# Attention on one core: context, input and weights transposed by the host, all batches written out, and a new spread of the projection steps

## The reference, cut to what matters

```python
# x [16, 256, 128], ctx_768 [16, 1601, 96]; 16 heads of 8
def self_attention(x, qkv_w, out_w, out_b):        # stage 1, keys = the batch's own 256 rows
    ...
    return jnp.einsum('bne,fe->bnf', out, out_w) + out_b
def cross_attention(x, context, ...):              # stages 2 and 5, keys = 1601 rows of the context
    q = x @ Wq.T + bq ; k, v = split(context @ Wkv.T + bkv)
    att = softmax(einsum('blhd,bmhd->blmh', q, k) * scale, axis=2)
    out = einsum('blmh,bmhd->blhd', att, v).reshape(b, l, d)
    return out @ Wo.T + bo
x = layernorm(x + self_attention(x))
x = layernorm(x + cross_attention_0(x, ctx_768))
x = layernorm(x + experts(x))
x = layernorm(x + state_space(x))
x = layernorm(x + cross_attention_1(x, ctx_768))
x = layernorm(x + feed_forward(x))
```

## Time and profile before

| | us |
|---|---|
| median of 3 runs | 4210.55 (4205.43 to 4215.28) |
| the profiled execution | 4211.14 |
| its span | 4209.1 |
| PE busy (matmul) | 3603.7 (86%) |
| DVE busy | 2896.4 (69%) |
| ACT busy | 2384.8 (57%) |
| POOL busy | 1032.1 (25%) |
| mean share of the 16 DMA engines, queue q1 | 19.7% |

### The profile page before, as it was taken

The page is one execution under the profiler, slowest core; times in us unless marked ns, Lnnn a source line. Parts: engine busy times, 40 slices in busy tenths (PEclk is TensorE's granted clock), DMA queues, the critical chain, the costliest instruction groups (busy, mean ns, idle before and its releaser), DMA issues. The chain is left out here.

```text
span 4209.1 us, 109822 instructions
## 1 busy us (share of the span) xinstructions
PE 3603.7 (86%) x39651; PEld 1800.8 (43%) x39651; DVE 2896.4 (69%) x3938; ACT 2384.8 (57%) x4687; POOL 1032.1 (25%) x1818
## 2 busy tenths in 40 slices
PE   4777599999999999997699583999999999999987
PEld 2444244343343434443466482443444334344435
DVE  4555677777777777784544696777777777777753
ACT  2444266666666666675233440666666666666663
POOL 3333232122222321221366102122212212221200
PEclk7889699999999999998799796999999999999998
DMA  2222222222222223221000002222222222222200
GB/s 73 57 54 53 58 56 55 68 60 53 60 51 51 56 53 73 59 50 27 1 0 0 1 0 49 59 51 56 56 69 60 52 60 50 52 55 67 55 21 20
DMA packets 222502, 200.19 MB, mean 48 GB/s; under 512 B 86918, under 2 KB 184444, under 8 KB 221964
## 3 DMA queue, kind: packets, MB, share of 16 engines
q1 hardware_dynamic: 221964, 193.04, 19.7%
HBM read 25.59 MB, written 2.10 MB: 7 GB/s over the span
## 5 line engine op out<-in xcount | busy, mean ns | idle before, releaser
L627 ACT ACTIVATE cross_Pr<-cross_sT 128x512 f32<-128x512 f32 (+1 forms) x3584 | 1833.4, 563 | 886.1 <-PE cross_sT L542 884.5
L691 DVE TENSOR_REDUCE cross_nm<-cross_ring 128x2 f32<-128x802 f32 x2048 | 1974.6, 991 | 492.5 <-PE cross_ring L508 482.7
L542 PE MATMUL cross_sT<-cross_Q,cross_K 64*128 64x256 bf16 x13312 | 1050.8, 274 | 111.3 <-ACT cross_Pr L627 40.7
L561 PE MATMUL cross_oT<-cross_Pr,cross_V 128*9 128x256 f32 x13312 | 1038.7, 383 | 0.6 <-issue 0.6
L542 PEld LDWEIGHTS cross_sT<-cross_Q,cross_K 64*128 64x128 bf16 x13312 | 514.1, 95 | 869.3 <-ACT cross_Pr L627 694.7
L508 PE MATMUL cross_ring<-cross_K,cross_Q 64*128 64x401 bf16 x4096 | 666.4, 338 | 38.3 <-DVE cross_nm L691 17.2
L436 POOL TENSOR_TENSOR cross_mp<-cross_nm,cross_one 128x8 bf16<-128x8 f32 x128 | 26.0, 203 | 1471.0 <-DVE cross_nm L696 1470.8
L561 PEld LDWEIGHTS cross_oT<-cross_Pr,cross_V 128*9 128x9 f32 x13312 | 198.4, 88 | 427.7 <-issue 247.3
L508 PEld LDWEIGHTS cross_ring<-cross_K,cross_Q 64*128 64x128 bf16 x4096 | 200.5, 94 | 170.6 <-DVE cross_nm L691 113.7
L700 DVE TENSOR_REDUCE self_nm<-self_ring 128x4 f32<-128x1024 f32 x128 | 156.7, 1224 | 141.2 <-PE self_ring L515 141.1
L1243 DVE TENSOR_TENSOR moe_rc<-moe_r,moe_bank 128x512 f32<-128x512 f32 x128 | 87.9, 687 | 169.3 <-ACT moe_r L1134 169.3
(11 more groups left out here) (326 smaller groups left out, 3370.8 us busy)
## 6 DMA issues: line engine op xcount, KB each, us to landing
cross_K<-cross_kparts SPq DMA_DIRECT2D x1152, 100.1 KB, 2.3
cross_C<-in_ctx_dram SPq DMA_DIRECT2D x32, 576.0 KB
cross_Q<-cross_qparts SPq DMA_DIRECT2D x288, 64.0 KB, 2.1
self_Q<-self_qparts SPq DMA_DIRECT2D x144, 64.0 KB, 2.1
self_K<-self_kparts SPq DMA_DIRECT2D x144, 64.0 KB, 2.1
cross_xs<-X SPq DMA_DIRECT2D x32, 128.0 KB, 2.1
X<-in_x_dram SPq DMA_DIRECT2D x4, 512.0 KB, 6.1
self_xs<-X SPq DMA_DIRECT2D x16, 128.0 KB, 2.1
```

The lines of the kernel that those rows point to most:

```text
L542: mm = pe.matmul(sT[0:r, cfg.sT_bank(rb, u + j), (c % 2) * S:(c % 2 + 1) * S], K[ROWS * j:ROWS * (j + 1), pair, t, s:s + r], Q[ROWS * j:RO ...
L561: mm = pe.matmul(oT[32 * j:32 * j + VR, 0:S], V[0:r, rb % VB, c, 4 * g + j, :], Pr[0:r, slot, (c % 2) * S:(c % 2 + 1) * S], start=(c == 0) ...
L627: act.activation(Pr[0:r, u % NPR, 0:nc_ * S], sT[0:r, cfg.sT_bank(rb, u), 0:nc_ * S], ACT.Exp).then_inc(exped, 1)
L691: dve.tensor_reduce(nm4[:, g % 2, t, :, pk, blk], R.rearrange("p (j n) -> p j n", j=2)[:, :, 0:cfg.block], AX.X, ALU.max, negate=True).the ...
```

## The change

1. **Layouts.** The host hands in `x_T` [16, 128, 256] and `ctx_T` [16, 97, 1601] (96 rows of the transposed context and a row of ones) and the weights already permuted, with the bias rows of K and V appended. `CT`, the tiles `C`, `cT`, `xs` and the turning of weights are gone. `LOAD_C` is one DMA of 97 x 1601 floats into one of two buffers `in0`, `in1`; each row is 6404 bytes, and on both sides the access pattern is 97 rows by 1601 elements. `LOAD_C` of batch b waits for `V` of batch b-2. `wk` and `wv` of the cross stages arrive as 97 x 128. `XT` is left in the cross stages only, and reads X directly; in self, Q, K and V are computed from `in`.
2. **Output bias.** L584's matmuls are gone. The bias is loaded on all 128 partitions, and GpSimd adds it to X in a step `BIAS` (one tensor_tensor of 128 x 256 per batch); `OUT` waits for it.
3. **Written out.** The hardware loop is gone, and all iterations are written out.
4. **Self.** Q's and K's parts share one tile, and STACK_Q and STACK_K are one set of 9 DMAs of 128 KB. Q and K of a batch move to steps -2s-4 and -2s-3, the STACK to -2s; `A` stays at -s.
5. **Cross schedule.** `A`, `MT` and `ROWS` are one step earlier; K at 9, 11, 13 (was 9, 10, 11), V at 48, 52, 55 (was 28, 31, 34), Q at 4, STACK_K at 27, 30, 44, s+1 (was 26, 30, 44, s+1), `LOAD_C` at 27 as before.

The diff, cut to its core:

```diff
-            self.loop = (1, B - 3, 2)
...
-                out += [(g * u - u - 5 + a * u // 16, ("A", g, a)) for a in range(16)]
-                out += [(g * u - 3, ("MT", g)), (g * u - 2, ("ROWS", g))]
-            out += [(-s + 1 + n, ("CT", n)) for n in range(3)]
-            out += [(-s + 5, ("XT", 0)), (-s + 7, ("Q", 0)), (-s + 7, ("SPLIT_Q",))]
-            out += [(-s + 9 + n, ("K", n)) for n in range(3)]
...
-            out += [(-s + 28 + 3 * n, ("V", n)) for n in range(3)]
-            out += [(-s + 13, ("STACK_Q",))]
-            out += [(-s + at, ("STACK_K", g)) for g, at in enumerate((26, 30, 44, s + 1))]
-            out += [(-2 * s + 27, ("LOAD_X",)), (-2 * s + 27, ("LOAD_C",))]
-            end = 3
+                out += [(g * u - u - 6 + (a * u + 2) // 16, ("A", g, a)) for a in range(16)]
+                out += [(g * u - 4, ("MT", g)), (g * u - 3, ("ROWS", g))]
+            out += [(-s + 1, ("XT", 0)), (-s + 4, ("Q", 0)), (-s + 4, ("SPLIT_Q",)), (-s + 12, ("STACK_Q",))]
+            out += [(-s + at, ("K", n)) for n, at in enumerate((9, 11, 13))]
...
+            out += [(-s + at, ("V", n)) for n, at in enumerate((48, 52, 55))]
+            out += [(-s + at, ("STACK_K", g)) for g, at in enumerate((27, 30, 44, s + 1))]
+            out += [(-2 * s + 27, ("LOAD_C",))]
+            bias, ox, ont, fin, ln = 2, (32, s + 3), s + 5, s + 7, s + 9
...
-            out += [(-2 * s, ("XT", 0)), (-2 * s + 1, ("Q", 0)), (-2 * s + 1, ("SPLIT_Q",)), (-2 * s + 2, ("K", 0)),
-                    (-2 * s + 2, ("SPLIT_K", 0)), (-2 * s + 4, ("V", 0)), (-3 * s + 4, ("LOAD_X",)),
-                    (-2 * s + 3, ("STACK_Q",)), (-2 * s + 3, ("STACK_K", 0))]
-            end = 2
+            out += [(-2 * s - 4, ("Q", 0)), (-2 * s - 4, ("SPLIT_Q",)), (-2 * s - 3, ("K", 0)),
+                    (-2 * s - 3, ("SPLIT_K", 0)), (-2 * s + 2, ("V", 0)), (-3 * s - 3, ("LOAD_X",)),
+                    (-2 * s, ("STACK_K", 0))]
+            bias, ox, ont, fin, ln = 0, (2 * u + 2, 4 * u + 2), s + 4, s + 6, s + 7
...
-        C = sb("C", [P, NCHK, DC], F32) if cfg.cross else None
-        cT = sb("cT", [DC + 1, NK], F32) if cfg.cross else xT
+        sT_in = [sb(f"in{j}", [KD, NK], F32) for j in range(2)]
...
-                    elif op == "LOAD_C":
...
-                        sp.dma_start(C[:, 0:NK // P, :],
-                                     src[:, 0:full, :].rearrange("o (c p) f -> p (o c) f", p=P)).then_inc(ctx_in, 16)
-                        sp.dma_start(C[0:NK - full, NK // P, :],
-                                     src[:, full:NK, :].rearrange("o p f -> (o p) f")).then_inc(ctx_in, 16)
+                    if op in ("LOAD_X", "LOAD_C"):
+                        if b >= 2:
+                            sp.wait_ge(by["dve"], cfg.read(i, "V", (len(cfg.chunk_units) - 1,), off - 2))
+                        sp.dma_start(sT_in[b % 2][:, :], src_T[b]).then_inc(in_ready[b % 2], 16)
...
+                                    sp.dma_start(stacks[b % cfg.kbufs][r:P:DH, t, :, :, :],
+                                                 parts[:, qa:PARTS + ka + 1:PARTS + ka - qa, :])\
+                                      .then_inc(stacked_k[0], 16)
...
+                    if op == "BIAS":
+                        if cfg.cross:
+                            pool.wait_ge(by["act"], cfg.read(i, "XT", (0,), off))
+                        xb = X[:, QT * b:QT * (b + 1), :]
+                        pool.tensor_tensor(xb, xb, bo[:, :].unsqueeze(1).broadcast_to([P, QT, D]), ALU.add)\
+                            .then_inc(biased, 1)
```

More of the change, by code:

```diff
@@ L32 @@
 ONES_BF16 = 0x3F803F80
[L35 to L42, removed]
 class Attention:
@@ L118, in _schedule @@
             out.append((g * u + u + 1, ("EV", g)))
-        for half in range(2):
-            out.append((2 * u * (half + 1) + end, ("OX", half)))
-        out += [(s + end + 2, ("ONT", 0)), (s + end + 4, ("OUT", 0)), (s + end + 5, ("LN",))]
+        out += [(at, ("OX", half)) for half, at in enumerate(ox)]
+        out += [(ont, ("ONT", 0)), (bias, ("BIAS",)), (fin, ("OUT", 0)), (ln, ("LN",))]
         rank = {op: n for n, op in enumerate(("B", "A", "PV", "MT"))}
@@ L142, in count, with base, read @@
         return sum(who is None or self.reader[e[0]] == who for e in units)
-    def base(self, i, rep, who):
-        if isinstance(i, int):
-            return sum(self.count(self.ring(m), who) for m in range(self.first_it, i))
-        lo = self.loop[0]
-        return self.base(lo, lo, who) + (i - lo) * self.count(self.ring(lo), who)
-    def read(self, i, rep, op, index, off):
+    def base(self, i, who):
+        return sum(self.count(self.ring(m), who) for m in range(self.first_it, i))
+    def read(self, i, op, index, off):
@@ L284, in rows, with slot_free @@
             return cfg.chunks[c][1]
[L286 to L309 removed]
+        iterations = range(cfg.first_it, cfg.last_it + 1)
+        def slot_free(pe, i, k):
+            units = cfg.ring(i)[:k]
+            for m in range(i - 1, cfg.first_it - 1, -1):
+                if len(units) < 2:
+                    units = cfg.ring(m) + units
+            if len(units) >= 2:
+                who = cfg.reader[units[-2][0]]
+                pe.wait_ge(by[who], cfg.base(i, who) + cfg.count(cfg.ring(i)[:k], who) - cfg.count(units[-1:], who))
         def split(eng, src, dst, sm, at):
@@ L480, in body @@
+                        pe.matmul(R[:, 0:S], wq[:, :], (xT if cfg.cross else sT_in[b % 2])[:, :],
+                                  start=True, stop=True).then_inc(filled, 1)
                     elif op == "K":
@@ L533, in body @@
                             pe.wait_ge(max_rows[g], 16 * (b + 1))
-                        before = [x for x in (cfg.sT_before(rb, u), cfg.sT_before(rb, u + 1)) if x is not None]
+                        before = [x for x in (cfg.sT_before(b, u), cfg.sT_before(b, u + 1)) if x is not None]
                         if before:
```

409 lines of the change are left out of this document (154 added, 255 removed).

## The result

The changed kernel takes 4449.4 us (median of 4 runs, 4447.75 to 4457.05) against 4211.3 for the kernel before: a ratio of 1.057 (95% interval 1.0552 to 1.0588), so it is slower by 238 us. The forecast was 4395, in a range of 4250 to 4640. The profiled execution has a span of 4449.2 us, 240 more than before.

What follows compares the result with a forecast made beforehand. The prediction took PE with its pipeline of steps to bound the cross stages, 3046 of 4209.1 us. Its sum: 4211.1 - 106 (self) - 250 (cross batches) + 476 (load waits) + 64 (cross starts) = 4395 us, range 4250 to 4640.

Steps and rivals of the forecast that it cites:

- One engine, by equal shares: Cross context load: transfers split only into equal shares, and 97 is prime, so all 97 rows go to one engine.
- Its duration: Context load on one engine: 621.2 KB at 24.1 GB/s take 25.8 us; 21 us the shortest allowed.
- The wait: Cross, before B of group 3: PE stands 15.1 us because ROWS queues behind the load, in 14 batches a stage.
- the break-even of 11: Cross context load: a load of about 11 us breaks even; every us above it costs 28.
- A wait with its clock: Cross: each wait plus 2 us for low clock behind it is 17 us; +238 us a stage, +476 for both.
- The batch without the wait: Cross batch apart from the load: 84.1 us, between 81.3 and 86; -125 us a stage, -250 for both.
- the K spacing and the earlier ROWS: Cross batch: a step between K units saves 0.8 us, ROWS one step earlier 0.7 us.
- The starts: Starts of the cross stages: +28 us in cross0, +36 in cross1, +64 together; -13 with the load spread.
- Self: Self stage: the stack wait and its low clock go, batch 24.9 to 17.6 us; -106 us, or -30 if it returns.
- The spread load: First rival: the context load goes to 14 engines, 2 us, no stall; total 3842 us; chance 0.08.
- The second rival: Context load: one engine without queueing behind it, or much faster than 24; total about 3880 us; chance 0.06.
- The third: Third rival: the engine moves 16.3 GB/s for long rows too, 38.1 us a load; total 4790 us; chance 0.05.

Runs made afterwards that it cites:

- 44 and 53 rows: The changed kernel with the cross stages' context load as two transfers, of 44 and 53 rows: 4152.05 us, ratio 0.9871 to the kernel before.
- the split load: The changed kernel with the cross stages' context load as two transfers, 96 rows and one row: 3864.85 us, ratio 0.9188 to the kernel before.
- the old-spread run: The split load with the old cross schedule for A, MT, ROWS (one step later), K and V: 3866.92 us, against 3864.85 for the split load.
- V late: The split load with the cross stages' wk and wv loads also split, V at 48, 52, 55: 3859.5 us, ratio 0.9169 to the kernel before.
- V early: The V late kernel with V's units back at steps 28, 31, 34: 3840.57 us, ratio 0.9126 to the kernel before.
- the bias run: The split load with the output bias as matmuls on TensorE again and no BIAS step: 3901.31 us, ratio 0.9266 to the kernel before.

## Why the prediction was right

**One engine, by equal shares.** Right, shown by the packet left over (785 = 49 x 16 + 1), by the share of 0.06, and by 44 and 53 rows.

**Its duration.** 24.1 GB/s were taken, 25 are seen in the window in which it ran alone. The load in the start took 27.2 us from its issue to the K projection, for 25.8 and 2 of latency. The 21 us taken as the shortest load had no row behind it, and 25 GB/s give 24.8.

**The wait.** Right in place and kind, a little small: 15.1 expected, 16.5 measured in the mean, 40 us over 28 batches. In the period shown, the rows land 39.5 us after the issue of group 0's stack, where the sum had 36.4. One part is the issue of that stack, 6.98 us instead of 5.7; the rest, some 2 us, no row resolves. That they were needed at 21.3 was right (PE stopped at 1315.6, 21.5 us after). The same short sum shows at the shorter load: 15.2 less the break-even of 11 gives 4, and 7.2 were measured. So the load that could be hidden is some 8 us, not 11.

**A wait with its clock.** 476 us were expected for the 28 waits and the low clock behind them, 516 measured (the two stages of the changed kernel less those of the split load). Of these 463 are the wait; the 53 left are 1.9 a batch, for 2 taken. So the 40 us are the wait's alone.

**The batch without the wait.** 84.1 us expected, 84.0 measured with the split load; over the two stages 241 us less than before, for 250. The terms that make it up: the bias right (1.05); writing out 3.6 instead of 4.3, by the mean (89.4) over cross0's first 12 periods; and the K spacing and the earlier ROWS, 1.5 together, are 0.6 by the old-spread run, all of it ROWS. Two terms were too large. The wait for ROWS was taken off twice: the batch of 88.7 us that served as the base has none of it, and the sum took 0.7 off that base once more. And half of the K units' wait was to come back as time, 0.8; with the spacing the wait went, and the batch was shorter by 0.1 at most. One term was too small: 84.8 with the old spread is 4.6 below 89.4, and CT's matmuls and the bias are 3.1 of it, so 1.5 more came with the layouts. The sum had CT's matmuls and not the 47.1 us of waits in front of them that the earlier trace rows shows, 1.5 a batch; the K units' wait on DVE fell by (49.3 - 20.6) / 32 = 0.9 in the same step. Which of the two it is, no run shows. That the errors cancel, 1.5 against 1.5, is luck.

**The starts.** +28 and +36 expected, +31 and +41 measured. With the load spread they should have been -13 together and were about 0 (62.8 and 63.6 us from the normalisation before to the first score, against 66.7 and 58.9). The term left out is V's late place: from self's last normalisation to the first score it is 61.3 us with V late and 54.2 with V early, 7 us a start.

**Self.** 106 us expected, 108.5 measured, and that near only because errors cancel. A batch takes 18.1 us instead of 17.6, so twelve of them brought 83 and not 88; the first normalisation came 17.5 us earlier instead of 14, and the last batches gave 8.4 instead of 4. For the 1.4 us of XT and bias no row stood in the sum, and the bias run shows 0.1 us a batch for its part. The prediction named merging and earlier steps in one breath; the earlier steps are 11 of the 108.5.

**The whole.** From 4395 to 4449 are 54 us: 40 from the wait, 9 from the batch without it, 8 from the starts, and self 2.5 the other way.

**The rivals.** The spread load (3842) was the right price for the other world: the split load gave 3865, 14 of the 23 us from the starts. The second rival, no queueing, is refuted by the wait. The third, 16.3 GB/s, by the 25.

## What to carry to other kernels

Look at the outermost dimension of a large transfer before its size: a row of ones appended to 96 rows made the number prime and turned a transfer that nobody had noticed into 16.5 us of standstill a batch, 18.4 with the low clock behind it, while a separate transfer for that row costs 0.3 us of issuing. And a transfer with much slack of its own still has to be judged by what stands behind it in the queue. An average DMA share of 0.20 said nothing of it; one late 16 KB transfer did. And not every wait in a table is time: 0.6 us a batch of the K units' waits went with the spacing and shortened the batch by 0.1 at most, while the two waits of 1.7 us for ROWS made it longer by all of their 3.4.

## What the hardware showed that I had not expected

The engine that only issues transfers slows down behind the load as well: the nine transfers of group 1's stack took 13.54 us to issue in the period shown. In the split load, the answering rows are

```profile
1116.19 0.58 SPq L330 DMA_DIRECT2D cross_in<-in_ctx_T_dram  x1
1116.81 0.29 SPq L332 DMA_DIRECT2D cross_in<-in_ctx_T_dram  x1
1117.15 6.70 SPq L358 DMA_DIRECT2D cross_K<-cross_kparts  x9
```

6.70 us. At the start of cross0 the nine transfers of Q's stack, issued while the load of batch 0 ran, took even 15.78 us, and 5.70 with the load split. It goes with the queue and not with the busy engine: in the period shown with the load in ScalarE's queue, SP issued 18 stack transfers in 12.15 us, most of them while the load ran, and in the period behind it in 14.03; with the load split they take 6.92 + 6.70. How much of the changed kernel's wait is this? ACT had written group 3's maxima by 1312.4, and their rows were issued at 1315.16, 2.8 us later, 0.4 before PE stopped at 1315.6. At the usual 1.8 us to land they would have been 1.4 us late; the other 16.6 of the 18.0 us are the queue on the loaded engine.
